# Mixture-of-experts rows: the last two blocks added to their tokens in PSUM by one-hot products

## The reference, cut to what matters

```python
logits = jnp.einsum('btc,ce->bte', x, Wg)
probs = jax.nn.softmax(logits, axis=-1)
top_vals, top_idx = jax.lax.top_k(probs, TOP_K)
gates = (jax.nn.one_hot(top_idx, E, dtype=probs.dtype) * top_vals[..., None]).sum(-2)
h = jax.nn.relu(jnp.einsum('btc,ech->bteh', x, W1) + b1)
y = jnp.einsum('bteh,ehc->btec', h, W2) + b2
out = jnp.einsum('bte,btec->btc', gates, y)
```

## Time and profile before

| | us |
|---|---|
| median of 3 runs | 280.03 (278.56 to 289.09) |
| profiled execution, its own time | 281.16 |
| its span, first to last instruction | 279.4 |
| PE busy | 256.1 (92%) |
| DVE, ACT, POOL busy | 165.1, 120.2, 127.6 |

### The profile page before, as it was taken

One profiled execution on the slowest core, in us unless ns is written; L12 is line 12 of the kernel. 1 busy time (PEld: TensorE's weight loads), 2 busy tenths in 40 slices (PEclk: granted clock), 3 DMA queues, 4 the chain that ended last, 5 costly groups with the idle time before them and its releaser, 6 DMA issues.

```text
span 279.4 us, 6611 instructions
## 1 busy us (share of the span) xinstructions
PE 256.1 (92%) x2563; PEld 216.6 (78%) x2563; DVE 165.1 (59%) x491; ACT 120.2 (43%) x346; POOL 127.6 (46%) x193
## 2 busy tenths in 40 slices
PE   8898999998999999999999978999698889998990
PEld 8777679666999999999999637998576666677780
DVE  3777888873753133212320088799897656675874
ACT  4577869331344224432244004667542211663330
POOL 8753120327446756777331324769855100434311
PEclk9999999999999999999999997999999999999997
DMA  6999990162397999999200330000000000000002
GB/s 220 379 423 423 287 297 34 42 230 70 81 335 276 320 350 356 400 321 292 104 14 31 95 111 0 0 5 2 4 4 0 2 1 2 0 2 2 2 14 74
DMA packets 10114, 39.15 MB, mean 140 GB/s; under 512 B 1595, under 2 KB 5435, under 8 KB 7292
## 3 DMA queue, kind: packets, MB, share of 16 engines
q1 hardware_dynamic: 8163, 34.81, 34.8%
q0 software_dynamic: 1920, 3.93, 4.9%
HBM read 35.54 MB, written 3.19 MB: 139 GB/s over the span
## 4 chain that ended last, share of the span: by engine, by line
PE 68%; DVE 17%; DMA 5%; ACT 4%; issue 3%; POOL 1%; SPq 1%; POOLq 0%; DVEq 0%
PE ps L953 14%; PE ps L930 10%; PE ps L940 5%; PE ps L992 5%; PE ps L1176 4%; PE ps L1027 3%; DMA pat<-in_pat 3%; PE ps L1003 2%; PE ps L709 2%; PE ps L1014 2%; PE ps L835 2%; DVE s L1932 2%; PE ps L1038 1%; DVE st L1931 1%; DMA xs<-x_rows,from_row 1%
## 5 line engine op out<-in xcount | busy, mean ns | idle before, releaser
L652 POOL COPY v_bd<-v_f 32x192 f32<-32x192 f32 x64 | 22.4, 350 | 32.4 <-ACT v_f L1249 27.4
L1379 ACT ACTIVATE hid<-ps,w1t 128x128 f32<-128x128 f32 x72 | 19.9, 375 | 35.4 <-PE ps L941 31.8
L595 POOL DMA_INDIRECT y_rows<-ys,to_row x20 | 19.8, 988 | 27.0 <-DVE ys L1888 24.6
L565 POOL TENSOR_TENSOR rstd<-veps,neg_half 128x2 f32<-128x2 f32 (+1 forms) x16 | 10.6, 663 | 40.4 <-DVE veps L1711 40.3
L1866 DVE COPY xga<-ps 128x128 f32<-128x128 f32 x20 | 5.8, 291 | 38.3 <-PE ps L918 38.0
L589 POOL DMA_INDIRECT xs<-x_rows,from_row x20 | 19.7, 984 | 19.0 <-PE ps L918 9.6
L953 PE MATMUL ps<-w1t,hid 128*128 128x192 f32 x144 | 24.6, 326 | 0.0
L709 PE MATMUL ps<-w1a,consts 128*128 128x384 f32 (+1 forms) x68 | 23.0, 483 | 1.3 <-DVE h_tok L1693 1.3
L953 PEld LDWEIGHTS ps<-w1t,hid 128*128 128x128 f32 x144 | 23.3, 190 | 0.0
L1027 PEld LDWEIGHTS ps<-p1T,v_bd 128*64 128x64 f32 x384 | 16.1, 137 | 4.7 <-ACT p1T L1249 2.8
L709 PEld LDWEIGHTS ps<-w1a,consts 128*128 128x128 f32 x68 | 12.2, 189 | 9.4 <-DVE h_tok L1693 2.3
(11 more groups left out here) (310 smaller groups left out, 675.8 us busy)
## 6 DMA issues: line engine op xcount, KB each, us to landing
w1t<-in_wt SPq DMA_DIRECT2D x12, 1256.0 KB, 9.8
w1t_mid<-in_wt SPq DMA_DIRECT2D x3, 1256.0 KB, 10.6
w1t_top<-in_wt SPq DMA_DIRECT2D x3, 1256.0 KB, 11.0
pat<-in_pat SPq DMA_DIRECT2D x6, 496.0 KB, 7.6
w1t_low<-in_wt SPq DMA_DIRECT2D x2, 1256.0 KB, 7.2
w1a<-in_w1a SPq DMA_DIRECT2D x1, 1322.0 KB
y<-y_rows SPq DMA_DIRECT2D x6, 192.0 KB, 3.5
w1b<-in_w1b SPq DMA_DIRECT2D x1, 835.2 KB
```

Of the source, the lines that this page charges most:

```text
L595: pool.indirect_dma_start(io["y_rows"], bass.IndirectOffsetOnAxis(to_row[:, j:j + 1], 0), ys[:, b, :], None).then_inc(scattered[b], 16)
L652: pool.tensor_copy(dst, src).then_inc(v_placed, 1)
L1379: ins = act.activation(hid[:, j % 2, 128 * k:128 * k + 128], hidden_out(j, k), ACT.Relu, bias=weights(j)[:, B1_AT + k:B1_AT + k + 1])
```

## The change

The rows of the last two blocks, 18 and 19, no longer go through HBM. Instead:

- Blocks 0 to 17 are scattered as before. For blocks 18 and 19 POOL scatters rows of zeros to their places in `y_rows`, at block 10, so that loading `y_rows` yields nothing for them. SP waits for the scatters of blocks 0 to 17 and for the zeros, and then loads `y2`.
- The gates of the two blocks' slots are found by products (`gates_in_parts` on DVE at block 6, fourteen bf16 products `gates_by_slot` on PE behind block 9, `gates_found` on DVE at block 10), the float32 gate cut into three bf16 parts. `mixes` on DVE at block 14 writes for each of the two blocks a matrix `mix` of 128 slots by 7 x 128 tokens that holds a slot's gate at its token. `mix` lies where the weight buffer of block 13 was.
- Behind the last block PE computes `mix` transposed times `ys` for the 7 tiles and the 2 blocks (`combine`, 14 products of 128x192) into four PSUM banks. It takes the place of ten fillers; of the five further ones one is left, and two new ones stand behind the transposes.
- `x_tok` plus the gated loaded rows is now made ahead: pair 0 by DVE before the bias of block 19, pair 1 by DVE right behind it, pairs 2 and 3 by ACT (gate times row, in place) and POOL (sums). The norm's statistics then need one more instruction for a pair: the sum of `h_tok` and the pair's PSUM bank.
- POOL's two fills (`qT`, `xt_lo`) move behind the two reciprocal roots.

The diff, without declarations and indented eight places less:

```diff
@@ -47,6 +47,8 @@
+NMIX = 2
+FIRST_MIX = NBLK - NMIX
...
@@ -174,6 +177,10 @@
+    with ExitStack() as last_rows:
+        mix = sb("mix", [128, NMIX, TT, 128], scope=last_rows)
+        mix_row = sb("mix_row", [128, NMIX, 128], scope=last_rows)
+        mix_tile = sb("mix_tile", [128, NMIX, TT], scope=last_rows)
...
@@ -385,6 +400,21 @@
+MIX_BANK = [0, 1, 5, 7]
+def mix_out(t):
+    return ps[0:rows(t), MIX_BANK[t // 2], 256 * (t % 2):256 * (t % 2) + C]
+def mix_pair(pair):
+    t0, t1 = 2 * pair, min(2 * pair + 2, TT)
+    return ps[0:rows(t0), MIX_BANK[pair], :].rearrange("p (t c) -> p t c", c=256)[:, 0:t1 - t0, 0:C]
+def gate_out():
+    return ps[:, 4, 256:256 + 3 * NMIX]
@@ -494,8 +524,9 @@
+    sp.wait_ge(zeroed, 16 * NMIX)
-        sp.wait_ge(scattered[b], 16 * len(range(b, NBLK, YBUF)))
+        sp.wait_ge(scattered[b], 16 * len(range(b, FIRST_MIX, YBUF)))
@@ -605,13 +636,17 @@
             gather(j + XBUF + 2)
-        scatter(j)
+        if j < FIRST_MIX:
+            scatter(j)
         if 1 <= j < 9:
             split_wqk_ends()
+            for m in range(FIRST_MIX, NBLK):
+                pool.indirect_dma_start(io["y_rows"], bass.IndirectOffsetOnAxis(to_row[:, m:m + 1], 0),
+                                        v_bd[:, 0, :, :].rearrange("p b c -> p (b c)"), None).then_inc(zeroed, 16)
         if j == 11:
@@ -623,10 +658,25 @@
             fill(xpb[0:CB, :], 0.0, vbd_zero)
+    def add_rows(pair):
+        t0, t1 = 2 * pair, min(2 * pair + 2, TT)
+        n = rows(t0)
+        pool.wait_ge(rows_gated, pair - 1)
+        for k in range(TOPK):
+            ins = pool.tensor_tensor(h_tok[0:n, t0:t1, :], y2[0:n, t0:t1, k, :], (x_tok if k == 0 else h_tok)[0:n, t0:t1, :], ALU.add)
+            if k == 0:
+                ins.then_inc(rows_half, 1)
+                pool.wait_ge(rows_half, pair - 1)
+            else:
+                ins.then_inc(rows_pool, 1)
+    add_rows(2)
+    add_rows(3)
     pool.wait_ge(y_ready, NBLK)
+    rsqrt(1, range(2))
     fill(qT[:, :, :, HALF:HALF + 8], 0.0, vbd_zero)
     fill(xt_lo[CB:128, :].bitcast(F32), 0.0, vbd_zero)
-    rsqrt(1, range(2))
@@ -715,9 +765,6 @@
             if layer == 2 and t == 0:
-                pe.wait_ge(summed, 1)
-                keep_busy(3, 4, 384)
-                pe.wait_ge(summed, 2)
                 keep_busy(3, 1, 384)
@@ -963,6 +1010,27 @@
+    def gates_by_slot():
+        pe.wait_ge(gate_lists, 1)
+        pe.wait_ge(xg_done, 33)
+        for i in range(PICKS):
+            n = rows(i % TT)
+            mm = pe.matmul(gate_out(), in_row[0:n, i, :], gate_ids[0:n, i, :, :].rearrange("p b v -> p (b v)"), start=(i == 0), stop=(i == PICKS - 1))
+        mm.then_inc(gate_found, 1)
+    def combine():
+        pe.wait_ge(mix_ready, NMIX)
+        for pair in range(PAIRS):
+            for m in range(NMIX):
+                if pair == 0:
+                    pe.wait_ge(ys_done, FIRST_MIX + m + 1)
+                for t in range(2 * pair, min(2 * pair + 2, TT)):
+                    mm = pe.matmul(mix_out(t), mix[:, m, TT - 1 - t, 0:rows(t)], ys[:, (FIRST_MIX + m) % YBUF, :],
+                                   start=(m == 0 and t % 2 == 0), stop=(m == NMIX - 1), skip_group_check=True)
+            mm.then_inc(mixed, 1)
@@ -975,6 +1043,8 @@
             pe.wait_ge(from_ready, 2)
+        if j == 10:
+            pe.wait_ge(gate_read, 1)
         if j + 2 < NBLK:
@@ -982,7 +1052,9 @@
             moved_ids()
-    keep_busy(2, 10, 384)
+        if j == 8:
+            gates_by_slot()
+    combine()
@@ -1058,6 +1130,7 @@
     to_channels(2, 4, range(4))
+    keep_busy(3, 2, 384)
     pe.wait_ge(wlate_in, 32)
@@ -1379,6 +1452,15 @@
+    act.wait_ge(picks_gated, 1)
+    for pair in (2, 3):
+        act.wait_ge(y2_in[pair], 16 * TOPK)
+        for t in range(2 * pair, min(2 * pair + 2, TT)):
+            n = rows(t)
+            for k in range(TOPK):
+                ins = act.activation(y2[0:n, t, k, :], y2[0:n, t, k, :], ACT.Copy, scale=pick_at[0:n, 1, TT * k + t:TT * k + t + 1])
+        ins.then_inc(rows_gated, 1)
@@ -1684,14 +1766,12 @@
         if layer == 1:
-            dve.wait_ge(y2_in[pair], 16 * TOPK)
-            for t in range(t0, t1):
-                ins = dve.scalar_tensor_tensor(h_tok[0:n, t, :], y2[0:n, t, 0, :], pick_at[0:n, 1, t:t + 1], res[0:n, t, :], ALU.mult, ALU.add)
-            ins.then_inc(y2_half, 1)
-            dve.wait_ge(y2_half, pair + 1)
-            for t in range(t0, t1):
-                ins = dve.scalar_tensor_tensor(h_tok[0:n, t, :], y2[0:n, t, 1, :], pick_at[0:n, 1, TT + t:TT + t + 1], h_tok[0:n, t, :], ALU.mult, ALU.add)
-            ins.then_inc(summed, 1)
+            if pair < 2:
+                dve.wait_ge(rows_dve, pair + 1)
+            else:
+                dve.wait_ge(rows_pool, pair - 1)
+            dve.wait_ge(mixed, pair + 1)
+            dve.tensor_tensor(h_tok[0:n, t0:t1, :], mix_pair(pair), h_tok[0:n, t0:t1, :], ALU.add).then_inc(summed, 1)
         elif layer == 0:
@@ -1856,7 +1936,48 @@
-        dve.tensor_reduce(as_picks(pick_at[:, 1, :]), picked[:, :, :, :], AX.X, ALU.add)
+        dve.tensor_reduce(as_picks(pick_at[:, 1, :]), picked[:, :, :, :], AX.X, ALU.add).then_inc(picks_gated, 1)
+    def gates_in_parts():
+        gate = pick_at[:, 1, :]
+        dve.wait_ge(picks_gated, 1)
+        link(dve.tensor_copy(gate_part[:, 0, :], gate))
+        link(dve.tensor_tensor(gate_rest[:, 0, :], gate, gate_part[:, 0, :], ALU.subtract))
+        link(dve.tensor_copy(gate_part[:, 1, :], gate_rest[:, 0, :]))
+        link(dve.tensor_tensor(gate_rest[:, 1, :], gate_rest[:, 0, :], gate_part[:, 1, :], ALU.subtract))
+        link(dve.tensor_copy(gate_part[:, 2, :], gate_rest[:, 1, :]))
+        dve.tensor_tensor(gate_ids[:, :, :, :], over(one_hot_of(MOVED)[:, :, FIRST_MIX - E:NDYN], 3),
+                          view(gate_part[:, 0, 0:1], [[1, PICKS], [0, NMIX], [PICKS, 3]]), ALU.mult).then_inc(gate_lists, 1)
+    def gates_found():
+        dve.wait_ge(gate_found, 1)
+        dve.tensor_reduce(slot_gate[:, :], gate_out().rearrange("p (b v) -> p b v", v=3), AX.X, ALU.add).then_inc(gate_read, 1)
+    def mixes():
+        dve.wait_ge(gate_read, 1)
+        for m in range(NMIX):
+            j = FIRST_MIX + m
+            link(dve.tensor_scalar(mix_row[:, m, :], iota_row, found[:, j, 0:1], slot_gate[:, m:m + 1], ALU.is_equal, ALU.mult))
+            link(dve.tensor_scalar(mix_tile[:, m, :], over_base[:, 1:E], found[:, j, 1:2], None, ALU.is_equal))
+            dve.tensor_tensor(mix[:, m, :, :], view(mix_row[:, m, 0:1], [[0, TT], [1, 128]]), over(mix_tile[:, m, :], 128), ALU.mult).then_inc(mix_ready, 1)
+    def add_rows(pair):
+        t0, t1 = 2 * pair, min(2 * pair + 2, TT)
+        n = rows(t0)
+        dve.wait_ge(y2_in[pair], 16 * TOPK)
+        for k in range(TOPK):
+            for t in range(t0, t1):
+                ins = dve.scalar_tensor_tensor(h_tok[0:n, t, :], y2[0:n, t, k, :], pick_at[0:n, 1, TT * k + t:TT * k + t + 1],
+                                               x_tok[0:n, t, :] if k == 0 else h_tok[0:n, t, :], ALU.mult, ALU.add)
+            if k == 0:
+                ins.then_inc(y2_half, 1)
+                dve.wait_ge(y2_half, pair + 1)
+            else:
+                ins.then_inc(rows_dve, 1)
@@ -1873,11 +1994,19 @@
             moved_rows()
+        if j == 10:
+            gates_found()
+        if j == 14:
+            mixes()
         if j % 2 == 0 and j + 2 < NBLK:
             gates_of_picks()
+        if j == 6:
+            gates_in_parts()
+        if j == NBLK - 1:
+            add_rows(0)
         if j == 15:
@@ -1886,6 +2015,7 @@
         dve.tensor_tensor(ys[:, j % YBUF, :], ps[:, Y_BANK[j % 2], 0:C], weights(j)[:, B2_AT:B2_AT + C], ALU.add).then_inc(ys_done, 1)
+    add_rows(1)
     for half in (range(2), range(2, PAIRS)):
```

More of the change, by code:

```diff
@@ L119, in build @@
         tri, every, iota128, ids = (col(moec_h, MOEC[:4], n) for n in ("tri", "every", "iota128", "ids"))
+        iota_row = col(moec, MOEC, "iota128")
         thresholds, before, over_base = (col(moec, MOEC, n) for n in ("thr", "before", "over"))
@@ L228, in build @@
         to_row = sb("to_row", [128, NBLK], I32, scope=ffn)
+        gate_part = sb("gate_part", [128, 3, PICKS], BF16, scope=ffn)
+        gate_rest = sb("gate_rest", [128, 2, PICKS], scope=ffn)
+        gate_ids = sb("gate_ids", [128, PICKS, NMIX, 3], BF16, scope=ffn)
+        slot_gate = sb("slot_gate", [128, NMIX], scope=ffn)
         xs = sb("xs", [128, XBUF, C], scope=ffn)
@@ L299, in build @@
         y2_half = sem("y2_half")
+        picks_gated, gate_lists, gate_found, gate_read = sem("picks_gated"), sem("gate_lists"), sem("gate_found"), sem("gate_read")
+        mix_ready, mixed, zeroed = sem("mix_ready"), sem("mixed"), sem("zeroed")
+        rows_dve, rows_half, rows_pool = sem("rows_dve"), sem("rows_half"), sem("rows_pool")
+        rows_gated = sem("rows_gated")
         wqk_cast, wqk_split = sem("wqk_cast"), sem("wqk_split")
```

## The result

The changed kernel takes 276.93 us (median of 18 runs), the kernel before 279.23 us on the same chip; ratio 0.9916, 95% interval 0.989 to 0.9942. That is 2.3 us, where 274.0 and a step of 6.6 were forecast. The profiled execution took 279.27 us, its span is 277.4.

What follows compares the result with a forecast made beforehand. The prediction took a 12.3 us latency from last product to norm as the bound, half an HBM trip: -6.2 (rows, norm) + 0.3 (POOL) + 0.6 (loop) - 1.3 (clock) = -6.6, forecast 274.0 us, range 271.7 to 277.5.

Steps and rivals of the forecast that it cites:

- collision: Rival: POOL's first sum starts early and stalls DVE's last product-sum up to 0.96 us; 274.6 to 275.9; chance 0.17.
- a lost clock: Case where PE's clock still falls around the values, so the 1.3 us counted for it do not come back.
- a late ACT: Case where ACT starts scaling pair 2 1 us late, so POOL gives back 1.3 us instead of 0.3.
- Fillers and clock: Two fillers between PE's transposes and values keep the clock at 2.4 GHz; 1.3 us gained, bounds 0 and 1.3.
- the clock falls all the same: Rival: PE's clock still falls near the transposes despite the fillers; step 5.3 us, time 275.3; chance 0.22.
- POOL before its roots: POOL's sums of pairs 2 and 3 delay its roots, so pair 1's `x_tok` comes 0.3 us later.
- Loads ahead: Loads wait for block 17's scatter only: pair 0's rows land at 152.62, all rows by 155.1.
- POOL's sums beside DVE's: DVE's PSUM sums and pair 1's product-sums are safe from POOL's sums; nothing counted.
- In the loop: Fourteen small PE products behind block 9 add 0.63 us; the DVE and POOL work added in the loop costs nothing.
- Sums ahead of the last bias: DVE's four pair 0 instructions run 153.20 to 154.76, before block 19's bias; no cost, by 0.09 us.
- Combine: PE's fourteen products take 4.6 us, 154.83 to 159.5, covered by DVE's own work.
- Behind it the pace is PE's again: After the first values PE sets the pace; POOL's second roots and DVE's later `x_tok` have less ahead than before.

Runs made afterwards that it cites:

- e7: The kernel before plus only the change's two fillers between the transposes and the values; 279.09 us, ratio 0.9986.
- e8: The kernel before plus the change's gate work alone, its results unused and the rows still going through HBM; 282.94 us, ratio 1.0081.
- e10: The changed kernel unedited, run again for a second profile and times; 277.32 us, ratio 0.991.
- e1: The changed kernel with POOL taking the roots of pairs 0 and 1 before its sums of pairs 2 and 3; 276.63 us, ratio 0.9883.
- e3: The changed kernel with the sums of pairs 2 and 3 back on DVE, without ACT's scaling and POOL's sums; 275.94 us, ratio 0.9885.
- e5: e1 with POOL's sums of pairs 2 and 3 also waiting until DVE has written `x_tok` of pair 1; 275.61 us, ratio 0.9848.
- e9: e5 with the short pair's sums on DVE behind its `x_tok` of pair 1, without ACT's scaling of that pair; ratio 0.9832.
- e11: e9 run again unedited, for its times; ratio 0.9828.

## Why the prediction was wrong

The forecast was -6.2 + 0.3 + 0.6 - 1.3 = -6.6. Measured: -2.3. The time, 276.93, lies near the high end of 277.5, for which the prediction had put a collision, a lost clock and a late ACT together; all three came, the collision in another place. By its own steps:

*Fillers and clock* failed, and is the step that was wrong in kind. It counted 1.3 us for a fall of the clock that the profiled run of before had. That run, 281.16 us at a clock of 0.986, was no typical one: of the 68 runs of before beside the experiments 37 had 0.990 to 0.993 and a median of 278.99, seven 0.986 to 0.987 and 279.89; its loop also began 1.2 us later than e7's (75.44 against 74.24), which the fall has nothing to do with. e7 and e8 show the stretch without a fall, and e7 that keeping PE busy there wins nothing. The change makes a fall of its own instead: five of its 30 runs had a clock of 0.994 or 0.995 (275.3 to 275.8), fourteen 0.989 to 0.990 (median 276.93), and e10, one of these, has the fall behind its gap (2.87 us there, 2.33 in after). The late norm makes that gap: where pair 0's `x_tok` came early (e1, e3, e5, e9, e11) PE waited at most 1.0 us at a time there, and PEclk is 1.00 through the values. The rival "the clock falls all the same" was right on the clock, and its 275.3 still assumed that all the rest of the step, 5.3, would come.

*POOL before its roots* was right as a mechanism and was mis-sized: 0.3 was counted, and the norm came 2.35 us late (9.42 us from the last bias to the end of `x_tok`; the forecast's steps give 161.25 + 0.67 - 154.85 = 7.07). In after, with the 0.18 taken off by which its last bias is later, POOL's sums start 1.46 later than forecast (158.49 - 0.18 against 156.85), take 3.25 instead of 2.95, the roots 1.48 instead of 1.4, and the last `x_tok` instruction ran 0.90 instead of 0.37 beside POOL's fill: 1.46 + 0.30 + 0.08 + 0.53 = 2.37.

The root of it is *Loads ahead*: "all rows in by 155.1" took the end of the traffic for the arrival, and put that end too early (its last window, 163 to 163.5 in the earlier trace rows, still has a share of 0.89). Pair 0 came in time, as forecast. But ACT was released for pair 2 at 156.91 and not at 155.1, although the DMA share is 0.08 in 156 to 156.5. The Trainium skill (Perfetto Trace Analysis, "DMA Instruction — HWDGE (DVE, Sync)") says that the last descriptor of a DMA issued by SyncE makes sure that the write is complete before the semaphore moves; the trace agrees, with 0.4 us or more from the end of the traffic (before 156.5) to ACT's start. SP's eight issues also took 5.03 us instead of 3.91. Over the ten profiles with early loads DVE waited 0 to 0.98 us for pair 1: this term varies from one execution to the next.

*POOL's sums beside DVE's*: DVE's product-sums were safe, as forecast, and so was the PSUM sum that ran beside POOL's sums (0.55). But "I count nothing" overlooked DVE's TENSOR_SCALAR, which stood 0.92 instead of 0.17 for `veps`, and in e1 2.22 instead of 0.67; in e5, where POOL's sums wait for it, it took 0.67 again. That is why e1 won only 0.22 us beyond the fall that it does not have: the order of POOL's queue and the lock are two ways of paying the same. The Trainium skill (SBUF — State Buffer, "Who interferes with whom") names `tensor_scalar` among the operations that can take the port pair shared with GpSimd; the prediction had used that section for two-input instructions only. The traces agree.

*In the loop*: 0.63 forecast, 0.78 measured (e8, and after: 155.03 - 75.02 = 80.01). *Sums ahead of the last bias* and *Combine* held: pair 0's sums run from 153.29 to 154.82, then DVE waits 0.21 us for PE and not the other way round; `combine` took 4.90 us for 4.6, under DVE's work.

*"Behind it the pace is PE's again"* holds for after (10.28 us from the values to the second half; 10.60 and 10.59 in e7 and e8, the runs of before's stretch without a fall). It would not have held had the norm come when forecast: e5 has it 6.88 us after the bias, and pays 12.27.

Put together from the table, against a run of before without a fall: norm 9.42 - 12.96 = -3.54, second half 10.28 - 10.60 = -0.32, loop +0.78: -3.1. The runs of the change at its highest clock agree (275.6 against the 279.0 of before at 0.990 to 0.993, -3.4), though none of them was profiled. The change's own fall returns 0.8 to 1.2 in its two profiles, which leaves 1.9 to 2.3. e9 removes the order, the lock, the fall and more than half of the second half's wait (11.10 against 12.27 in e5 and 10.28 in after), and its fastest runs are where the forecast was, near 274.

## What to carry to other kernels

Before counting a fall of the clock as a gain, set the profiled run's clock beside those of the timed runs: a loss that the profile shows may be one that the typical run does not have. When work is moved to an idle engine's queue, price the instructions already behind it by the arrival of the slowest input, read at a consumer that waits for it and not at the end of the traffic. And when a first half is brought forward, follow the second half's chain before counting the gain.

## What the runs showed of the hardware that was not expected

A DVE TENSOR_SCALAR of 128x2 took 0.92 us beside a POOL sum instead of 0.17; two of 128x192 took 2.22 instead of 0.67; one beside a POOL MEMSET took 0.90 instead of 0.37, and in e3 two took 1.20 instead of 0.67 beside the same MEMSET. POOL's sums did not slow down (0.99 each), its MEMSET a little (0.86 instead of 0.76), and statistics and sums with an operand in PSUM ran undisturbed (0.62, 0.55). The same gap of 1.38 us on PE was followed by a fall of the clock in one execution of before and by none in e8.
